# A batched matmul with gathered matrices: first loads in larger transfers, a shorter warm-up, and half of batch 1 turned by VectorE

## The reference

```python
Tb = T[itok - 1]
out = x + jnp.einsum('bij,bjk->bik', Tb, x)
```

## Time and profile before

| | |
|---|---|
| median of 3 runs | 114.21 us (112.63 to 115.53) |
| the profiled execution | 112.17 us, span 110.4 us |
| TensorE (PE) busy | 103.9 us, 94% of the span |
| VectorE, GpSimd, ScalarE busy | 79.9, 73.0, 66.3 us |
| mean granted TensorE clock | 0.992 of full speed |
| DMA | 25.29 MB, mean 229 GB/s |

### The profile page before, as it was taken

One profiled execution on the slowest core, in us unless ns is written; L12 is line 12 of the kernel. 1 busy time (PEld: TensorE's weight loads), 2 busy tenths in 40 slices (PEclk: granted clock), 3 DMA queues, 4 the chain that ended last, 5 costly groups with the idle time before them and its releaser, 6 DMA issues.

```text
span 110.4 us, 1810 instructions
## 1 busy us (share of the span) xinstructions
PE 103.9 (94%) x496; PEld 86.9 (79%) x496; DVE 79.9 (72%) x89; ACT 66.3 (60%) x86; POOL 73.0 (66%) x38
## 2 busy tenths in 40 slices
PE   4998999997999999999999999999999999999960
PEld 4997778885888778888888888888888888888850
DVE  0353964664989976999699978998799869932250
ACT  1825686855397757595759575957595858522220
POOL 2000559994849996998599949994999499940000
PEclk9999999999999999999999999999999999999996
DMA  1789999366998998999899899905930062006254
GB/s 71 215 225 327 376 393 224 112 198 159 365 211 271 401 287 233 317 388 275 262 307 382 243 284 313 388 27 172 425 163 0 0 276 107 0 6 285 98 227 153
DMA packets 15996, 25.29 MB, mean 229 GB/s; under 512 B 1778, under 2 KB 11250, under 8 KB 14322
## 3 DMA queue, kind: packets, MB, share of 16 engines
q10 hardware_dynamic: 2450, 14.81, 36.2%
q1 hardware_dynamic: 13536, 10.36, 34.1%
HBM read 16.78 MB, written 8.39 MB: 228 GB/s over the span
## 4 chain that ended last, share of the span: by engine, by line
PE 78%; DVE 7%; DMA 5%; POOL 4%; ACT 2%; issue 1%; POOLq 0%; DVEq 0%; ACTq 0%
PE same L430 23%; PE diff L441 22%; PE same L423 21%; PE turned L406 5%; DMA x_sb<-x 5%; PE diff L392 3%; PE same L397 3%; POOL xL L281 3%; DVE xL L313 2%; DVE TL L348 1%; DVE out_sb L356 1%; DVE xD L324 1%; ACT xH L192 1%; DVE out_sb L383 1%; DVE TL L342 1%
## 5 line engine op out<-in xcount | busy, mean ns | idle before, releaser
L281 POOL TENSOR_TENSOR xL<-x_sb,xH 128x1024 fp32r<-128x1024 f32 x14 | 33.7, 2408 | 10.3 <-ACT xH L192 10.3
L219 ACT ACTIVATE diff<-same 128x512 f32<-128x512 f32 x31 | 18.0, 582 | 28.5 <-PE same L430 28.5
L430 PE MATMUL same<-xL,TL 128*128 128x512 f32 x128 | 34.9, 392 | 0.2
L294 POOL TENSOR_TENSOR TD_r<-TH_r,TL 128x1024 fp32r<-128x1024 f32 x14 | 33.8, 2413 | 1.7 <-DVE TL L348 1.7
L423 PE MATMUL same<-xH,TH_r 128*128 128x512 f32 x128 | 34.6, 392 | 0.0
L441 PE MATMUL diff<-xD,TD_r 128*128 128x512 f32 x124 | 34.0, 396 | 0.0
L356 DVE TENSOR_TENSOR out_sb<-x_sb,diff 128x512 f32<-128x512 f32 x31 | 21.2, 683 | 14.8 <-PE diff L441 14.7
L430 PEld LDWEIGHTS same<-xL,TL 128*128 128x128 f32 x128 | 23.9, 188 | 6.3 <-POOL xL L281 0.5
L423 PEld LDWEIGHTS same<-xH,TH_r 128*128 128x128 f32 x128 | 23.8, 188 | 4.9
L441 PEld LDWEIGHTS diff<-xD,TD_r 128*128 128x128 f32 x124 | 22.8, 189 | 4.3
L324 DVE SCALAR_TENSOR_TENSOR xD<-xL,xH_copy 128x1024 fp32r<-128x1024 f32 x16 | 19.3, 1208 | 2.1 <-POOL xL L281 1.4
(11 more groups left out here) (20 smaller groups left out, 24.4 us busy)
## 6 DMA issues: line engine op xcount, KB each, us to landing
out<-out_sb ACTq DMA_DIRECT2D x7, 1024.0 KB, 7.8
x_sb<-x ACTq DMA_DIRECT2D x6, 1024.0 KB, 7.4
T_sb<-T SPq DMA_DIRECT2D x72, 64.0 KB, 4.6
T_sb<-T SPq DMA_DIRECT2D x14, 256.0 KB, 5.8
x_sb<-x SPq DMA_DIRECT2D x6, 256.0 KB, 5.9
x_sb<-x ACTq DMA_DIRECT2D x2, 256.0 KB, 3.3
out<-out_sb ACTq DMA_DIRECT2D x1, 512.0 KB, 2.6
out<-out_sb SPq DMA_DIRECT2D x1, 256.0 KB, 2.6
```

Source lines behind the costliest of these rows:

```text
L219: nc.scalar.activation(diff[U % 2][:], same[U % 2][:], COPY, scale=-(RADIX + 1.0)).then_inc(seeded, 1)
L281: nc.gpsimd.tensor_tensor(half(xL, h), x_sb[b % X_SLOTS][:, i:i + 2], half(xH, h).bitcast(fp32), ALU.subtract).then_inc(xL_ready, 2)
L294: nc.gpsimd.tensor_tensor(TD_r[s][:], TH_r[s][:].bitcast(fp32), TL[s][:].bitcast(fp32), ALU.subtract).then_inc(TD_ready, 2)
L430: done = nc.tensor.matmul(same[U % 2][:], TL[p][:, i, j], xL[s][:, j], start=False, stop=(j == N - 1))
```

## The change

x[0] comes in two transfers of 512 KB (two blocks each, runs of 4 KB), both on ScalarE's queue; where TensorE turns, T comes in transfers of two blocks; x[1] is one transfer of 1 MB. SyncE therefore issues T[0] in two transfers, x[1], and then the later T's. `WARM` is 7. In batch 1 TensorE turns units 4 and 5 and VectorE units 6 and 7, behind sum_up(2). T[1]'s blocks 2 and 3 come in four pieces of 64 KB each. ScalarE cuts x blocks 2 and 3 before T's unit 0, and VectorE makes xL(2) and xL(3) before TL(0).

```diff
--- before.py
+++ after.py
@@ -26,8 +26,8 @@
     X_SLOTS, T_SLOTS, X_SETS, T_SETS, OUT_SLOTS = 4, 3, 3, 4, 2
     RADIX = 4096.0
     LEAN = 1.0 - 0.5 / RADIX
-    BY_PE = [N, N] + [1] * (B - 2)
-    WARM, REWARM = 14, 2
+    BY_PE = [N, N // 2] + [1] * (B - 2)
+    WARM, REWARM = 7, 2
     HALVES = [slice(0, D // 2), slice(D // 2, D)]
 
     x_part = x.rearrange("b (p u) k -> b p u k", u=N)
@@ -65,7 +65,7 @@
         eye_step = sem("eye_step")
         itok_loaded = sem("itok_loaded")
         x_loaded = [sem(f"x_loaded{s}") for s in range(X_SLOTS)]
-        first_x_loaded = [sem(f"first_x_loaded{n}") for n in range(N)]
+        first_x_loaded = [sem(f"first_x_loaded{i}") for i in range(2)]
         T_loaded = [[sem(f"T_loaded{s}_{n}") for n in range(N)] for s in range(T_SLOTS)]
         turned_by_pe = sem("turned_by_pe")
         turned_by_dve = sem("turned_by_dve")
@@ -115,12 +115,18 @@
             if turns_by_dve(U):
                 eng.wait_ge(turned_by_dve, turns_by_dve(U))
 
+        def T_transfers(b):
+
+            pe = BY_PE[b]
+            return {n: (min(n + 2, pe), 1) for n in range(0, pe, 2)} | {n: (n + 1, G) for n in range(pe, N)}
+
         def wait_T_loaded(eng, U):
             b, n = U // N, U % N
             s = b % T_SLOTS
-
-            before = sum(1 if by_pe(c * N + n) else G for c in range(s, b + 1, T_SLOTS))
-            eng.wait_ge(T_loaded[s][n], 16 * before)
+            first = max(f for f in T_transfers(b) if f <= n)
+
+            count = sum(T_transfers(c)[first][1] for c in range(s, b + 1, T_SLOTS) if first in T_transfers(c))
+            eng.wait_ge(T_loaded[s][first], 16 * count)
 
         def half(tiles, h):
             return tiles[h // 2 % X_SETS][:, 2 * (h % 2):2 * (h % 2) + 2]
@@ -128,20 +134,17 @@
         def load_x(eng, b, tiles=slice(0, N)):
             eng.dma_start(x_sb[b % X_SLOTS][:, tiles], x_part[b, :, tiles]).then_inc(x_loaded[b % X_SLOTS], 16)
 
-        def load_first_x(eng, n):
-            eng.dma_start(x_sb[0][:, n], x_part[0, :, n]).then_inc(first_x_loaded[n], 16)
-
-        def load_T(eng, t, b, blocks):
+        def load_T(eng, t, b):
             s = b % T_SLOTS
-            for n in blocks:
-                if by_pe(b * N + n):
-                    eng.dma_start(T_sb[s][:, n], T_rows[bass.ds(t, 1), :, n].rearrange("a p j -> (a p) j")
+            for n, (end, pieces) in T_transfers(b).items():
+                if pieces == 1:
+                    eng.dma_start(T_sb[s][:, n:end], T_rows[bass.ds(t, 1), :, n:end].rearrange("a p n j -> (a p) n j")
                                   ).then_inc(T_loaded[s][n], 16)
-                else:
-                    for g in range(G):
-                        eng.dma_start(T_sb[s][g * Q:(g + 1) * Q, n].rearrange("q (m c) -> q m c", m=G),
-                                      T_part[bass.ds(t, 1), n, g].rearrange("a q m c -> (a q) m c")
-                                      ).then_inc(T_loaded[s][n], 16)
+                    continue
+                for g in range(G):
+                    eng.dma_start(T_sb[s][g * Q:(g + 1) * Q, n].rearrange("q (m c) -> q m c", m=G),
+                                  T_part[bass.ds(t, 1), n, g].rearrange("a q m c -> (a q) m c")
+                                  ).then_inc(T_loaded[s][n], 16)
 
         def store(eng, b, tiles, done, cols=slice(0, D)):
             eng.dma_start(out_part[b, :, tiles, cols], out_sb[b % OUT_SLOTS][:, tiles, cols]).then_inc(done, 16)
@@ -156,18 +159,14 @@
                 return sp.snap(t, min_val=0, max_val=K - 1)
 
             t = matrix(itok_row[0:1, 0:1])
-            load_T(sp, t, 0, [0])
-            for n in range(2, N):
-                load_first_x(sp, n)
-            load_T(sp, t, 0, range(1, N))
-            for n in range(N):
-                load_x(sp, 1, slice(n, n + 1))
+            load_T(sp, t, 0)
+            load_x(sp, 1)
             sp.wait_ge(itok_loaded, 16)
             for b in range(1, B):
                 t = matrix(itok_sb[0:1, b:b + 1])
                 if b >= T_SLOTS:
                     wait_turned(sp, (b - T_SLOTS + 1) * N)
-                load_T(sp, t, b, range(N))
+                load_T(sp, t, b)
             sp.wait_ge(sum_ready, UNITS - 1)
             store(sp, B - 1, slice(N - 2, N - 1), last_stored)
             sp.wait_ge(sum_ready, UNITS + 1)
@@ -179,12 +178,12 @@
         @block.scalar
         def _(act):
             def cut_first_x(u):
-                act.wait_ge(first_x_loaded[u], 16)
+                act.wait_ge(first_x_loaded[u // 2], 16)
                 nc.scalar.activation(xH[0][:, u], x_sb[0][:, u], COPY, scale=LEAN).then_inc(xH_ready, 1)
 
             def cut_x_half(h):
                 b = h // 2
-                act.wait_ge(x_loaded[b % X_SLOTS], 64 if b == 1 else 16 * ((b - 1) // X_SLOTS + 1) + 48 * (b % X_SLOTS == 1))
+                act.wait_ge(x_loaded[b % X_SLOTS], 16 * ((b - 1) // X_SLOTS + 1))
                 if b >= X_SETS:
 
                     act.wait_ge(same_ready, (b - X_SETS + 1) * N)
@@ -222,15 +221,15 @@
                 for bank, cols in zip(last_diff, HALVES):
                     nc.scalar.activation(bank[:, cols], same[U % 2][:, cols], COPY, scale=-(RADIX + 1.0)).then_inc(seeded, 1)
 
-            for n in range(2):
-                load_first_x(act, n)
+            for i in range(2):
+                act.dma_start(x_sb[0][:, 2 * i:2 * i + 2], x_part[0, :, 2 * i:2 * i + 2]).then_inc(first_x_loaded[i], 16)
             act.dma_start(itok_sb[:], itok_row).then_inc(itok_loaded, 16)
             cut_first_x(0)
             cut_first_x(1)
             copy_xH_half(0)
-            cut_T(0)
             cut_first_x(2)
             cut_first_x(3)
+            cut_T(0)
             copy_xH_half(1)
             cut_T(1)
             for k in range(PAIRS):
@@ -377,6 +376,7 @@
                     cut_T_pair(p)
                 sum_up(2 * k)
                 for p in T_pairs(k)[1:]:
+                    turn_pair(p)
                     cut_T_pair(p)
             for i, cols in enumerate(HALVES):
                 dve.wait_ge(last_diff_ready, i + 1)
```

## The result

The changed kernel takes 113.56 us in the median of 20 executions (112.99 to 114.71), the kernel before 112.62 us in 20 (111.81 to 115.53). The ratio is 1.0097 with a 95% interval of 1.0070 to 1.0123: 1% slower, and clear of the noise. The forecast was no change with a small gain (113.9 against 114.21, a ratio of 0.997). That 113.9 lies so near to the measured 113.56 is luck: it starts from 114.21, the median of three executions, where twenty give 112.62. The profiled execution of the changed kernel took 113.48 us with a span of 111.7, 1.3 us more than the span before.

What follows compares the result with a forecast made beforehand. It took one dense matmul stream on TensorE as the bound, gated midway by pair 3's turn. Start -2.2 and pair +1.92 gave -0.3 us, so 113.9 us against 114.21; range 112.2 to 116.7, its own 112.8 to 115.9.

Steps and rivals of the forecast that it cites:

- What bounds the kernel, and where the change meets it: Dense matmul stream behind the start; turn of pair 3 gates both turn(8) and x[2]'s issue; 3.6 us idle ahead of turn(8).
- The term of the pair: Middle: VectorE turns units 6 and 7 behind sum_up(2), so TH starts at 27.09 in place of 25.17: +1.92 us.
- The start: Up to the first products: earlier turn(0), xL cuts not slowed, TL(1) in time: -2.2 us, between -3.0 and -1.2.
- T's landing: Start: T's first 512 KB lands at 8.0 us, between 7.2 and 9.0, and decides when turn(0) starts.
- The warm-up: Start: with WARM 7 its 14 records end at about 7.1 us, 8.2 if all slow, no longer holding turn(0).
- The step that failed: Middle: 3.6 us idle ahead of turn(8) counted by length alone, four 512-column matmuls behind it still taking 0.91 us.
- rival 1: Clock falls in the gap ahead of turn(8): +2.3 us, +2.0 in total, 116.2 us; chance 0.25.
- The price of the clock: Behind the gap ahead of turn(8): work worth 2.3 us lost in the next 4.6 if the clock falls.
- x[2]'s chain: From pair 3's cut over x[2]'s transfer to 38.96: moves by the same amount as turn(8)'s stream, leaving no cover.
- I count 0: Wait of some 0.3 us at 38.96 could vanish, or x[2] land up to 1 us later; priced 0.
- the lower end: Forecast's own range from T's landing and x[2], -1.1 to +1.7 us, given as 112.8 to 115.9 us.

Runs made afterwards that it cites:

- e7: Changed kernel with x[2] issued at the head of k = 1 and twelve unit-matrix products filling the gap ahead of turn(8): 112.15 us, ratio 0.996 to the kernel before.
- e5: Changed kernel, but TensorE turns all of batch 1 and x[2] is issued at the head of k = 1: 110.45 us, ratio 0.978 to the kernel before.
- e9: Kernel before with WARM 7, the new order of cuts and x[2] early, so e5 with the old 256 KB first transfers: 111.70 us, ratio 0.991.
- e3: Changed kernel with twelve unit-matrix products on TensorE in the gap ahead of turn(8): 112.70 us, ratio 1.001 to the kernel before.
- e6: Changed kernel with only x[2] issued early, at the head of k = 1: 113.82 us, ratio 1.011 to the kernel before.
- e1: Changed kernel, but TensorE turns all of batch 1 again: 111.09 us, ratio 0.985 to the kernel before.
- e13: e5 with x[0]'s blocks 0 and 1 as 256 KB each and blocks 2 and 3 issued behind itok: 112.78 us, ratio 0.994 to the kernel before.
- e14: e12 with x[0]'s blocks 0 and 1 as 256 KB each and blocks 2 and 3 issued behind itok: 114.59 us, ratio 1.016 to the kernel before.
- e15: The same kernel as e12, run again for one profiled execution: 112.16 us.
- e2: Kernel before with only VectorE's turn of units 6 and 7 added (64 KB pieces): 116.62 us, ratio 1.038.
- e10: e5 with x[0]'s second half issued by SyncE behind T's first transfer instead of by ScalarE: 113.58 us, ratio 0.998 to the kernel before.
- e4: Changed kernel with unit 8's turn moved on TensorE behind diff(3) and same(5): 112.23 us, ratio 0.996 to the kernel before.
- e12: Changed kernel with x[2] issued early and VectorE turning units 6 and 7 ahead of sum_up(2): 110.55 us, ratio 0.981 to the kernel before.

## Why the prediction was wrong

The forecast was a small gain, and the measured change is a loss. The rival that had been given one chance in four, the clock, is what made the sign.

**What bounds the kernel, and where the change meets it: right.** The forecast put the change's cost at the turn of pair 3, behind sum_up(2), and named both things that hang on it. The trace after shows two transposes from 23.09 to 25.16, TL to 27.62 and TensorE idle for 3.50 us (forecast 3.6).

**The term of the pair: right in size.** +1.92 forecast; +1.74 between the two traces and 1.70 between e7 and e5.

**The start: right in kind, 0.5 us too large.** -2.2 forecast, -1.65 measured. T landed at 8.2 (forecast 8.0) and the first x cut began at 4.59 (4.5). That T's landing fits so well is in part luck. The rate was what the forecast took (0.89 MB in 3.1 us is 287 GB/s, and 289 were moved from 4.90 to 8.90), and more than it counted had moved ahead of 4.90 (282 GB/s in place of 202). But the index load, for which the forecast had no term, made T's issue 1.5 us later. The warm-up ended at 8.0 and not at 7.1 (its 14 records took 2.89 us from 5.11, the slow pace of the earlier trace rows nearly to the end); T hid that. The parts by themselves, each taken back from e5: transfers 1.4 us, order of cuts 0.9, warm-up 0.5. They add up to more than the start gained, so they are not terms of one sum, and the first has a fall of the clock in it (e9).

**The step that failed: the sum took the gap ahead of turn(8) at its own length, with the matmuls behind it "then still at 0.91 us for four".** The forecast saw a gap five times as long as any in the rows, knew from the warm-up that TensorE starts slow, and still left the clock out of its sum, as rival 1. The clock fell: 0.57 from 27.70 to 31.70, and four matmuls took 1.71 us. That alone cost about 1.6 us. With the clock held up and nothing else changed the ratio is 1.001 (e3), which is what the rest of the sum had said: about no change. e3 and e7 show that the idle stretch is the cause: the same wait, with products in it that compute nothing, leaves the clock at 1.00. The Trainium skill, "TensorE: Matmul & The Clock Gate", section "What's actually happening", has an idle array return to the throttled state; the trace agrees, with TensorE idle for 3.50 us and then a clock of 0.57. With 3.6 us of idle time forecast, the clock's price belonged in the sum.

**The price of the clock: forecast 2.3 us, measured 1.67** (e6 - e7), and 1.6 by the trace of the changed kernel. The forecast took half of the 4.6 us that TensorE had needed at the start; the slow stretch here lasted about 3.4.

**x[2]'s chain: right, and more than was said.** The forecast said that both paths move together and left no cover. So filling the gap alone gives 0.9 us (e3), and e1 runs into x[2] in its profiled execution. The wait at 38.96, for which "I count 0" stood, did vanish, and gave 0.4 us back. That x[2]'s transfer would vary from 5.3 to 7.5 us was in no term.

**The total.** -1.65 + 1.74 + 1.21 = +1.3 us between the profiled executions; +0.9 between the medians. With the failed step put right (+1.67 on -0.3) the forecast would have been +1.4. One slip in its working changes nothing here: a change of -1.1 on 114.21 gives 113.1 us, and the 112.8 given as the lower end belongs to -1.4.

What stays open: what decides whether the clock falls behind an idle stretch of about 2 us (it fell in e13, e14's start and e15, and not in e5 or at e14's turn(8)); why T's first block lands later when it is issued earlier (e13); and why the DMA engines at a share of 0.97 move 209 GB/s at 6 to 8 us and 383 just after. The runs don't tell.

## What to carry to other kernels

A wait on TensorE has two prices, its own length and the slow stretch behind it; where a change opens a gap of microseconds in a dense stream, put the clock into the sum, and give the work back to TensorE (e5) or hold the gap short (waits of 2.0 to 2.4 us went either way here), before trusting to fillers (e7). Moving 1 us of work off the busiest engine gains nothing if the receiver does it later and slower on the chain: ask what has to be done before it on the receiver. And a load issued behind a wait inherits that wait: x[2] needed nothing that pair 3 made.

## What the runs showed of the hardware

- The clock fell after 3.50 us without matmuls (in the changed kernel, e2 and e6) and after 2.18 us in one execution (e15) but not in another (e14). At the start it fell behind waits of 3.31 (e9), 2.56 (e10), 2.35 (e13) and 2.04 us (e14), and not behind 2.02 (e5). In the traces it did not fall behind the 0.74 us of the kernel before, nor behind the 1.49 us of e1 and e4.
- SyncE's load of one integer from DRAM took 0.49 to 0.55 us with 256 KB transfers ahead of it, 1.27 with one of 512 KB, and 1.7 to 2.1 with two (1.1 in e12's trace, where it began 1.2 us later).
- The granted clock reads 1.00 in the first microseconds, when TensorE is at half pace; there only the durations (421 and 275 ns in the earlier trace rows) tell.
- VectorE's xL, with both operands in SBUF, went from 0.69 to 1.79 us beside GpSimd's TD, and that one from 1.30 to 1.67. VectorE's xD, with one operand in PSUM, kept its 1.22 us beside GpSimd's TD (10.71 and 10.46 in the changed kernel).
